# Delta rule: all four diagonal blocks of the state copied by ScalarE instead of two by VectorE and two by ScalarE

## The reference

```python
x = x + _L0_attn_a_ref(_layernorm(x), ...)      # Mamba
x = x + _L0_ffn_ref(_layernorm(x), ...)         # mixture of experts
x = x + _L0_attn_b_ref(_layernorm(x), ...)      # delta rule
x = x + _L0_ffn_ref(_layernorm(x), ...)         # mixture of experts
```

```python
def step(S, inp):
    qi, ki, ui, wi = inp
    attn_i = jnp.where(tri_incl, qi @ jnp.swapaxes(ki, -1, -2), 0.0)
    ui = ui - wi @ S
    oi = qi @ S + attn_i @ ui
    S = S + jnp.swapaxes(ki, -1, -2) @ ui
    return (S, oi)
```

## Time and profile before

| what | value |
|---|---|
| median of 3 runs | 1907.61 us (1902.32 to 1911.67) |
| profiled execution | 1913.05 us |
| span of its instructions | 1911.3 us |
| mean granted TensorE clock | 0.797 |
| busy in the span: TensorE, VectorE | 1281.5 us (67%), 1305.3 us (68%) |
| busy in the span: ScalarE, GpSimd | 917.3 us (48%), 1079.4 us (56%) |

### The profile page before, as it was taken

One profiled execution on the slowest core, in us unless ns is written; L12 is line 12 of the kernel. 1 busy time (PEld: TensorE's weight loads), 2 busy tenths in 40 slices (PEclk: granted clock), 3 DMA queues, 4 the chain that ended last, 5 costly groups with the idle time before them and its releaser, 6 DMA issues. The chain is left out here.

```text
span 1911.3 us, 31174 instructions
## 1 busy us (share of the span) xinstructions
PE 1281.5 (67%) x12628; PEld 595.0 (31%) x12628; DVE 1305.3 (68%) x1605; ACT 917.3 (48%) x1702; POOL 1079.4 (56%) x464
## 2 busy tenths in 40 slices
PE   4484948758495675844478774657778777748875
PEld 1121413222131322211134331324444545423332
DVE  3789899999989899899670022477778776635002
ACT  4566564847565474754232202545666644323220
POOL 1899999999999799999610001143434455430000
PEclk9686968778695887966789886778898887768978
DMA  5927274472818337271199972121233222239997
GB/s 129 212 57 192 50 187 112 115 184 57 218 44 199 80 96 192 57 193 49 40 397 421 421 288 80 36 46 38 52 80 79 68 58 70 57 117 392 422 421 273
DMA packets 193695, 299.88 MB, mean 157 GB/s; under 512 B 82704, under 2 KB 125200, under 8 KB 177168
## 3 DMA queue, kind: packets, MB, share of 16 engines
q1 hardware_dynamic: 188512, 295.17, 50.8%
q10 hardware_dynamic: 4688, 2.19, 0.4%
q0 software_dynamic: 352, 0.52, 0.1%
HBM read 255.37 MB, written 42.47 MB: 156 GB/s over the span
## 5 line engine op out<-in xcount | busy, mean ns | idle before, releaser
L376 POOL TENSOR_TENSOR state<-dx_rep,b_rep 128x2048 f32<-128x2048 f32 x128 | 578.5, 4523 | 63.3 <-PE psum L744 30.0
L608 DVE TENSOR_TENSOR_SCAN psum<-psum,state 128x1024 f32<-128x1024 f32 x160 | 365.2, 2283 | 25.6 <-POOL state L376 13.7
L744 PE MATMUL psum<-state,sel 128*32 128x512 f32 x1024 | 190.5, 841 | 264.5 <-POOL state L385 234.9
L491 ACT ACTIVATE psum<-delta_rep,a_neg 128x511 f32<-128x511 f32 x512 | 330.7, 679 | 60.6 <-DVE state L608 60.4
L608 DVE TENSOR_TENSOR_SCAN state<-psum,state 128x1024 f32<-128x1024 f32 x96 | 218.7, 2279 | 36.0 <-ACT psum L491 36.0
L385 POOL TENSOR_TENSOR state<-state,c_rep 128x1024 f32<-128x1024 f32 x96 | 225.5, 2350 | 0.0
L615 DVE TENSOR_TENSOR state<-psum,c_rep 128x1024 f32<-128x1024 f32 x160 | 195.8, 1224 | 5.5
L668 PE MATMUL psum<-xt,w_in 128*128 128x512 f32 x256 | 132.0, 664 | 41.3 <-ACT z_silu L458 25.6
L744 PEld LDWEIGHTS psum<-state,sel 128*32 128x32 f32 x1024 | 28.8, 129 | 395.4 <-issue 275.3
L488 ACT COPY psum<-zeros 128x2 f32<-128x2 f32 x160 | 25.8, 161 | 236.1 <-DVE state L615 226.7
L1873 PE MATMUL psum<-xt_delta,w_qkv 128*128 128x512 f32 x192 | 116.8, 749 | 11.9 <-DVE conv_qkv L1650 8.3
(11 more groups left out here) (226 smaller groups left out, 2425.4 us busy)
## 6 DMA issues: line engine op xcount, KB each, us to landing
moe_w_set<-in_w SPq DMA_DIRECT2D x30, 4096.0 KB, 34.0
delta_rep<-delta_scratch SPq DMA_DIRECT2D x128, 256.0 KB, 5.4
dx_rep<-dx_scratch SPq DMA_DIRECT2D x128, 256.0 KB, 7.9
b_rep<-bc_scratch SPq DMA_DIRECT2D x32, 256.0 KB, 4.8
delta_scratch<-delta SPq DMA_DIRECT2D x32, 256.0 KB, 7.7
c_rep<-bc_scratch SPq DMA_DIRECT2D x32, 256.0 KB, 8.0
moe_x<-x_after SPq DMA_DIRECT2D x16, 512.0 KB, 9.0
moe_w_set<-in_w SPq DMA_DIRECT2D x4, 2048.0 KB, 32.4
```

The source lines that it names most:

```text
L376: nc.gpsimd.tensor_tensor(ring[q % RING][:, :, :], dx_rep[u % CHUNKS][:, :, :], free_bcast(b_rep[q // QPB % 2][:, g, :], 1, CB), ALU.mult) ...
L491: ins = nc.scalar.activation(dec[:, i, 1:], delta_rep[u % CHUNKS][:, c, 1:], ACT.Exp, scale=a_neg[:, dt * CB + c, g:g + 1])
L608: nc.vector.tensor_tensor_scan(bx if by_pool(k) else flat, flat, bx, 0.0, ALU.mult, ALU.add).then_inc(S["scan_done"], 1)
L744: ins = nc.tensor.matmul(bank[32 * c:32 * c + 32, :], sel[:, :], ring[q % RING][:, c, :], start=False, stop=(g == NG4 - 1), skip_group_che ...
```

## The change

ScalarE copies all four blocks in its phase 2 and then raises s_ready_act; VectorE copies none and no longer waits for s_psum; the semaphore s_ready and TensorE's two waits for it go. Nothing else is moved: the slot, the data, the source and the destination stay the same.

```diff
--- before.py
+++ after.py
@@ -1254,7 +1254,7 @@
             "conv_done", "qk_feat", "v_feat", "sq_ready", "stat_psum", "stat_ready", "stat_t_psum", "ssq_ln", "gate_exp",
             "norms", "gate_one", "gate_ready", "one_minus_g", "lam_ready", "g1_ready", "lam_mask", "tok_psum", "tok_ready",
             "vn_ready", "vg_ready", "gram_psum", "n_read", "attn_read", "n_stored", "n_loaded0", "n_loaded1", "solve", "solve_pool", "t_stored",
-            "t_loaded0", "t_loaded1", "t_scaled", "vn_psum", "x_chunk", "y_ready", "u_psum", "u_ready", "s_psum", "s_ready", "s_ready_act", "o_psum", "o_read",
+            "t_loaded0", "t_loaded1", "t_scaled", "vn_psum", "x_chunk", "y_ready", "u_psum", "u_ready", "s_psum", "s_ready_act", "o_psum", "o_read",
             "o_added", "o_sq", "o_ms", "o_ln", "o_r", "o_scaled", "ot_psum", "ot_ready", "res_loaded", "out_psum",
             "out_added", "x_stored")}
         SOLVE = 2 * (HC - 1) + 5
@@ -1527,7 +1527,7 @@
                                 ins.then_inc(S["u_ready"], 1)
                             if phase == 2 and k % SPG != SPG - 1:
                                 act.wait_ge(S["s_psum"], leaving_state(k))
-                                for g in (2, 3):
+                                for g in range(HS):
                                     blocks, place = state_blocks(g)
                                     ins = nc.scalar.copy(place, blocks)
                                 ins.then_inc(S["s_ready_act"], 1)
@@ -1710,12 +1710,6 @@
                             k = CT * c + n
                             if phase == 0 and n:
                                 read_o(k - 1)
-                            if phase == 2 and k % SPG != SPG - 1:
-                                dve.wait_ge(S["s_psum"], leaving_state(k))
-                                for g in (0, 1):
-                                    blocks, place = state_blocks(g)
-                                    ins = nc.vector.tensor_copy(place, blocks)
-                                ins.then_inc(S["s_ready"], 1)
                         if tail is not None and m == 0:
                             read_o(CT * tail + CT - 1)
                         if turn is not None and m == at["ln"]:
@@ -1800,7 +1794,6 @@
                 def k_times_state(k):
                     w, n = k // CT, k % CT
                     feat = feats[w % COPIES]
-                    pe.wait_ge(S["s_ready"], leaving_state(k - 1))
                     pe.wait_ge(S["s_ready_act"], leaving_state(k - 1))
                     for hh in range(KD):
                         for p in range(NP):
```

## The result

The changed kernel takes 1917.99 us against 1908.37 us for the kernel before (medians of 18 runs each): a ratio of 1.005 with a 95% interval of 1.003 to 1.0071, or +9.5 us (+5.7 to +13.5). One execution of the changed kernel took 3833.73 us; the ratio leaves it out, and without it the median is 1917.76 us. Measured a second time it gives 1.0064 (1.0036 to 1.0092), +12.2 us. The forecast was +4.7 us, 1912.3 us. The time lies within the forecast range, but the effect lies at the half per cent that was put down as the limit of what can be told, not well inside it; of the rivals the first size of (2), +11.0 us, comes nearest.

What follows compares the result with a forecast made beforehand. ScalarE with TensorE was taken as the path without slack from period 4 on. Periods 1 to 6 +5.29, period 7 -1.66, period 8 +0.67 and +0.39: +4.7 us on 1907.61, so 1912.3 us; range 1900 to 1923.

Steps and rivals of the forecast that it cites:

- (2): Rival: ScalarE decides everywhere; first size +11.0 us (1918.6), second +20.1 us (1927.7) if all 30 steps lose; chance 0.19.
- The path: Delta-rule loop: ScalarE with TensorE, through token copy and statistics read L1584, has no slack to speak of from period 4 on.
- VectorE's relief: VectorE's dropped copies: 0.25 us at step 1 where its path decides, nothing at step 0 in periods 1 to 6.
- steps 2 and 3: Slots 10 and 14: ScalarE's added copies covered, except +0.39 us three times, in periods 5, 6 and 8.
- period 7: Seventh loop pass: VectorE sheds the pairs of steps 0 and 1 in its solve, -1.66 us; other gains lost before t_tok.
- period 8: Eighth loop pass, VectorE idle: +0.67 us in step 0, 0 in step 1, +0.39 in step 2.
- period 5: Fifth loop pass: TensorE has no slack for masks, so ScalarE's added time counts in full, +1.52 us.
- Period 6: Sixth loop pass: +1.52 us on both paths, as VectorE itself waits for ScalarE's gates; +1.91 with step 3 of period 5.
- ScalarE's 0.76 us: Price of ScalarE's second pair of copies, ahead of token copies in step 0 and of L1584 in step 1.
- The slack of TensorE: TensorE's mask waits at the second Gram half, 2.90, 0.38, 1.55, 0.18 us in periods 1 to 4, subtracted from ScalarE's addition.
- step-2 term: Period 8, step 2: four ScalarE copies release TensorE later, the third +0.39 us.
- step 0: Period 8: ScalarE's four copies end at 1664.54, where TensorE went on at 1663.93 before: +0.67 us.

Runs made afterwards that it cites:

- vector_relief: Changed kernel with ScalarE copying only blocks 2 and 3; nobody copies blocks 0 and 1: 0.999, -1.9 us (-5.9 to +2.3) against before.
- load_all: Kernel before plus two more ScalarE copies per step into an unread place, VectorE keeping its copies: 1.0054, +10.3 us (+6.1 to +14.5).
- units67: Kernel before with ScalarE copying all four blocks in periods 7 and 8 alone: 0.9998, -0.4 us (-5.2 to +4.4).
- units05: Kernel before with ScalarE copying all four blocks in periods 1 to 6, shared in 7 and 8: 1.0051, +9.7 us (+5.7 to +13.7).
- late01_split23: Kernel before, ScalarE copying all four in steps 0 and 1, behind token copies and L1584 with gates; steps 2, 3 shared: 0.9964, -6.9 us.

## Why the prediction was right in its path and wrong in its sum

**The path: right in periods 1 to 5.** Waits for masks gone (the forecast had left some in periods 1 and 3), waits for ScalarE longer, VectorE's relief worth little there, steps 2 and 3 next to nothing: all as forecast. That periods 1, 3 and 4 came within 0.3 us of their forecasts (+0.04, +0.05 and +1.6 against -0.25, -0.03 and +1.34) is in part luck, with traces of one kind up to 3 us apart there and a rule for the slack that didn't hold (below). The largest misses are period 7 (4.5 us), period 8 (2.5) and period 5 (2.3). Period 6 came out lower, +0.6 against +1.91, because there VectorE's relief did count: from the transposes of the statistics to the second Gram half 14.5 us became 13.0 to 13.3, and in vector_relief, which loads nothing on ScalarE, it is 13.35.

**ScalarE's 0.76 us: too high by 0.14.** TensorE's wait for L1584 went from 1.46 to 2.08 us, +0.62, in each of the periods 1 to 5. In the rows of after above, the first of the four copies starts at 1474.77, before L1501 ends (1474.18 + 0.67 = 1474.85); in the earlier trace rows the pair waited for that end. In load_all, where block 2 comes first again, the wait is 2.21 us, +0.75. That a copy beginning with block 0 may overlap the activation ahead of it, and one beginning with block 2 not, is what these rows show; why, was not tested.

**The slack of TensorE: the step that failed in periods 2 and 5.** The prediction took one execution's waits for masks as a property of each period. The repeat of before, TensorE's second Gram halves of periods 2, 3 and 4:

```profile
1381.44 0.79 PE L1915 MATMUL psum<-feat 32*32 32x64 f32 x59 [1.77 <-DVE attn_t L1695]
...
1437.33 0.90 PE L1915 MATMUL psum<-feat 32*32 32x64 f32 x70 [3.15 <-DVE attn_t L1695]
...
1493.53 1.47 PE L1915 MATMUL psum<-feat 32*32 32x64 f32 x128 [1.61 <-DVE attn_t L1695]
```

They are 1.77, 3.15 and 1.61 us where the earlier trace rows have 0.38, 1.55 and 0.18. Longer waits don't explain a larger loss, though: by the prediction's own rule, what ScalarE adds less TensorE's wait, they would have made it smaller. What failed is the rule that a wait swallows the added time one for one.

What doesn't vary is the distance from the transposes of the statistics (L1896) to the second Gram half: 16.54 or 16.55 us in the periods 1 to 4 of all three traces with shared copies, while the mean granted clock over that stretch was anything from 0.79 to 1.00. So in the kernel before VectorE sets a fixed length there, and a slower TensorE only shortens its own wait. With all four copies on ScalarE the same stretch takes 14.83 to 17.31 us, 15.94 in the mean. These 0.6 us are not VectorE's relief: load_all, in which VectorE keeps its copies, has 15.80 to 16.30 us, 15.97 in the mean, and no wait for masks in periods 2 to 5. The transposes, from which the stretch counts, come later there by ScalarE's copies, and the masks don't move with them: in load_all's period 1, where TensorE still waited 1.03 us for the masks, it is 15.80 us, 16.55 less the 0.75 that L1584 is later. Its periods 1 and 4 (L1901 is L1896, L1920 is L1915):

```profile
1311.96 0.55 PE L1901 MATMUL psum<-ident,stat_rows 96*128 96x96 f32 x4 [2.21 <-ACT stat_rows L1589]
...
1327.76 1.47 PE L1920 MATMUL psum<-feat 32*32 32x64 f32 x128 [1.03 <-DVE attn_t L1700]
...
1483.00 0.73 PE L1901 MATMUL psum<-ident,stat_rows 96*128 96x96 f32 x4 [2.21 <-ACT stat_rows L1589]
...
1498.90 0.82 PE L1920 MATMUL psum<-feat 32*32 32x64 f32 x60
```

The other part of the period, from the second Gram half to the next transposes, goes from 39.9 us in the mean (38.2 to 41.9) to 42.1 (39.2 to 44.5): +2.2 us, of which 0.62 us twice is ScalarE's. Most of the rest, 0.8 us, lies in the second Gram half itself: from its start to TensorE's next product with the state 1.86 us passed in the mean of periods 1 to 4 with shared copies, and 2.68 with all four. In these four periods of the six traces, where TensorE had waited 1.5 us or more for the masks, it paused at most 0.2 us within the half. Where it had waited less or not at all it paused 0.7 to 1.9 us, but for period 2, and the profile names nothing that it waited for ("issue"). In period 4 of the changed kernel:

```profile
1495.03 0.82 PE L1907 MATMUL psum<-feat 32*32 32x64 f32 x61 [1.16 <-issue]
```

So a part of the wait for masks that the change took away came back as this pause: 0.8 us of period 2's +1.8, 1.2 of period 5's +3.8. Why TensorE pauses there no run tested. Its clock doesn't make up the rest: from the second Gram half to the next transposes TensorE was busy for 30.1 us in the mean with shared copies and 30.2 with all four.

**Period 7: -1.66 us forecast, +2.9 found.** The term was the relief of VectorE in its solve. Behind six periods of the kernel before it brought nothing: units67 took 53.97 us against 53.60 and 53.75. VectorE from n_lane to the end of the solve took 25.98 us before (1621.52 to 1647.50) and 25.27 after (1620.71 to 1645.98): 0.71 us gained, not 1.66. Nearly all of the rest went back into one instruction behind the removed pair: 3.22 to 3.24 us in the seven traces in which VectorE copies its pair of step 1 there, 4.09 to 4.13 in the seven in which it doesn't. Before:

```profile
1637.23 3.23 DVE L1684 TENSOR_TENSOR prod<-t_lane,n_lane 128x2048 f32<-128x2048 f32 x1
```

After:

```profile
1620.71 0.16 DVE L1665 TENSOR_TENSOR prod<-t_lane,n_lane 128x2 f32<-128x2 f32 x1 [7.74 <-DMA n_lane<-n_scratch]
...
1634.82 4.13 DVE L1684 TENSOR_TENSOR prod<-t_lane,n_lane 128x2048 f32<-128x2048 f32 x1
```

The larger part came in with n_lane, which VectorE waited 7.74 us for. Within the stage n_lane arrived 10.4 us later than before, though TensorE came to the period's first product with t_tok only 7.5 us later. From the issue of n_lane to the next issue of t_scratch, period 6's solve on VectorE took 36.1 to 36.4 us in the three traces with shared copies and 37.4 to 38.4 in the others: +1.7 us, near the 1.52 that the prediction gave both paths in that period. Behind it SyncE's queue, which the prediction didn't cost, added as much. Its issues (start, duration of the issue), before:

```profile
1606.05 0.34 SPq L1358 DMA_DIRECT2D t_scratch<-t_lane  x1
1609.17 2.25 SPq L1364 DMA_DIRECT2D t_tok<-t_scratch  x4
1611.47 4.22 SPq L1370 DMA_DIRECT2D n_scratch<-squares_mask_gram  x4
1618.09 0.34 SPq L1377 DMA_DIRECT2D n_lane<-n_scratch  x1
```

After:

```profile
1601.97 0.34 SPq L1358 DMA_DIRECT2D t_scratch<-t_lane  x1
1606.46 3.38 SPq L1364 DMA_DIRECT2D t_tok<-t_scratch  x4
1609.88 2.53 SPq L1370 DMA_DIRECT2D n_scratch<-squares_mask_gram  x4
1616.23 0.34 SPq L1377 DMA_DIRECT2D n_lane<-n_scratch  x1
```

From t_scratch to n_scratch 5.42 us became 7.91; the other traces with shared copies have 5.3 and 5.7 us, the repeat of after 6.7 and units05 6.8. Of the store of t_scratch the last four packets landed alone. The DMA view of after, 1604.9 to 1606.3 us:

```profile
DMA packets 4, 0.01 MB, mean 9 GB/s; under 512 B 1, under 2 KB 1, under 8 KB 4
```

Why they come late there was not settled. And the waits that were removed came back under another name, as the prediction said of t_tok, and as it didn't say of VectorE's reads of o (L1701), which stand between the rows of the solve. TensorE after, period 7 and the start of 8, beside the earlier trace rows:

```profile
1628.50 1.08 PE L1812 MATMUL psum<-s_delta,feat 128*32 128x128 f32 x16 [6.92 <-DVE o_delta L1701]
...
1646.96 1.08 PE L1812 MATMUL psum<-s_delta,feat 128*32 128x128 f32 x16 [4.00 <-DVE o_delta L1701]
...
1658.31 0.98 PE L1827 MATMUL psum<-y_chunk,t_tok 32*32 32x32 f32 x64 [3.73 <-POOL t_tok L1489]
```

**Period 8: +1.06 us forecast, +2.3 and +4.9 found.** The step-2 term held: from the product of step 2 to that of step 3 TensorE took 6.30 us before, 6.65 after, +0.35 against 0.39. What failed is step 0, from the first product with t_tok to the next. Stretches of that step (bounds, length, busy us and instructions of TensorE and its weight loads, VectorE, ScalarE, GpSimd, then the granted clock, DMA share, GB/s). Before, and its repeat:

```profile
1659.61:1665.14 5.53, 3.91 (x178) 2.76 (x179) 2.36 (x4) 3.79 (x9) 2.25 (x1) 1.00 0.33 101
```

```profile
1649.92:1655.46 5.54, 3.91 (x179) 2.77 (x179) 2.37 (x4) 3.80 (x9) 2.25 (x1) 1.00 0.35 104
```

After, and its repeat:

```profile
1658.31:1665.77 7.46, 6.25 (x179) 4.11 (x179) 1.55 (x2) 4.52 (x11) 2.25 (x1) 0.54 0.26 75
```

```profile
1669.81:1677.41 7.60, 6.37 (x178) 4.23 (x179) 1.55 (x2) 4.53 (x11) 2.26 (x1) 0.50 0.25 73
```

units05, with shared copies there:

```profile
1665.01:1672.21 7.20, 5.96 (x179) 4.04 (x180) 2.47 (x4) 3.81 (x9) 2.25 (x1) 0.58 0.27 77
```

The same 179 products took 3.9 us of TensorE at a granted clock of 1.00, the 2.4 GHz level, and 6.0 to 6.4 us near 0.5, the 1.2 GHz level: about 2 us, not the 0.67 of the copies (and not the 3.3 us that the expectation for units67 put there). In the repeat of after the next step ran at 0.53 as well and took 8.31 us, where the other traces of this table have 5.87 to 5.93: the other half of its +4.9. In the two traces of before TensorE had waited 1.07 and 1.19 us for t_tok ahead of the stretch; in these three 3.73, 3.31 and 4.30. All fourteen traces go the same way: the two of before have the shortest waits and 1.00, the other twelve waited 1.51 us (load_all) to 4.30 and had 0.50 to 0.75. That the longer wait is what lost the clock is still argued, not shown, since no run changed it alone.

**The chances.** Rival 2 at its first size had a condition, TensorE's slack under 1.5 us in periods 1 to 3. In those periods the repeat of before shows waits of under 0.2, of 1.77 and of 3.15 us, and the table has +0.04, +1.8 and +0.05: the condition held in part, and the time came out at that rival's size for other reasons as well: the pause in the second Gram half, late n_lane and the clock of period 8. The 0.20 given to slower was too little for a sum in which SyncE's queue and the clock behind a longer wait had no price of their own: a chain without slack takes in whatever else is late.

The Trainium skill's advice to empty PSUM with both engines ("TensorEngine Tiling (Array Packing)", Performance Considerations, PSUM Bottleneck) agrees with the outcome: one engine's four copies took 1.48 us, the two engines' pairs 0.83. What mattered more here is the place in the queue: late01_split23 empties PSUM with ScalarE alone in steps 0 and 1 and is faster than the split of before.

## What to carry to other kernels

A wait of one engine for another, read from one execution, is not the slack of the path: look whether the distance between two events is fixed over periods and traces (16.55 us here), take the least of the waits, and look what else runs up to its end behind them: here a pause of TensorE showed itself once the wait was gone. Before moving work to another engine, list what stands behind it in that engine's queue and who waits for that; putting the work behind those instructions was worth more here than the choice of engine. And when an order loses its slack, cost the queues that it hands on to (here SyncE's store, load, store, load to the next n_lane), since nothing behind them gives the time back.

## What the runs showed of the hardware that was not expected

The same 128x2048 product on VectorE took 3.23 us in one kernel and 4.13 in the other, and 2.29 for the next product of that size, 6 us later, in both; by fourteen traces it is the longer one wherever VectorE's state copy ahead of it is missing. A first copy of partitions 0 to 31 began 0.09 to 0.12 us before the 128-partition activation L1501 ahead of it on ScalarE had ended, in each of ten places of the trace of after; one of partitions 64 to 95 began 0.02 or 0.03 us behind that end, in each of the ten places of before. From the issue of the store of 512 KB to the next issue in SyncE's queue 2.6 to 5.1 us passed in different periods and traces, with a few last packets landing one by one in the slow one that was looked at. And one kernel differs by place from one execution to the next: the same stretch of period 1 took 14.83 and 17.31 us in the two traces of the changed kernel, at granted clocks of 0.77 and 0.70; 0.9 us of the difference is TensorE's busy time, and 1.6 us a pause that only the second has and for which the profile names no cause.
